# Alternating two products on TensorE: the output product's head pairs and the values product's quarters in the local attention block

## The reference

```
bk2, bv2 = look(bk), look(bv)             # each window of 32 tokens sees itself and the one before
sim  = einsum('bhwie,bhwje->bhwij', bq, bk2) * QK_SCALE   # 16 heads of 64, after l2norm and rotary
attn = softmax(where(mask, -max, sim))
out  = einsum('bhwij,bhwje->bhwie', attn, bv2)             # the values product
x    = out.reshape(b, n, 1024) @ Wo + x                    # the output product
x    = ffn_layer(shift_tokens(x), ...) + x                 # layernorm, 128 -> 2 x 341 -> 128
```

## Time and profile before

| what | value |
| --- | --- |
| median of three timed runs | 4304.2 us |
| the profiled execution's own time | 4290.83 us |
| its span, first to last instruction | 4289.1 us |
| TensorE busy (matmul) | 4007.8 us, 93% |
| VectorE, GpSimd, ScalarE busy | 3256.0, 2944.0, 2597.3 us |
| granted TensorE clock, mean | 0.976 |
| stages loc0 and loc1 | about 1540 us each |

### The profile page before, as it was taken

How to read it: one execution, slowest core, us unless ns; L and a number is a source line. 1 busy time by engine, 2 the same in 40 slices (tenths; PEclk the granted TensorE clock), 3 DMA queues, 4 the chain that set the end, 5 groups by cost and what they waited for, 6 DMA issues and landing times. The chain is left out here.

```text
span 4289.1 us, 151479 instructions
## 1 busy us (share of the span) xinstructions
PE 4007.8 (93%) x66856; PEld 2950.2 (69%) x66856; DVE 3256.0 (76%) x3915; ACT 2597.3 (61%) x3040; POOL 2944.0 (69%) x3505
## 2 busy tenths in 40 slices
PE   8989969999999999999878887799999999999998
PEld 5655557787777787877633333677778777777775
DVE  4535568887888888888668884788888888887885
ACT  4525436666667667667537774466666666666664
POOL 2202168888888888888534441788888888888884
PEclk9999989999999999999989998899999999999999
DMA  4304233233333323322100000333323333232221
GB/s 154 123 10 155 96 100 85 72 88 83 80 84 86 82 76 90 89 66 76 40 11 1 1 1 8 113 81 81 87 79 85 85 85 86 75 87 75 75 65 41
DMA packets 169725, 316.93 MB, mean 74 GB/s; under 512 B 39336, under 2 KB 43056, under 8 KB 166640
## 3 DMA queue, kind: packets, MB, share of 16 engines
q1 hardware_dynamic: 153520, 241.18, 20.7%
q0 software_dynamic: 15552, 66.07, 5.0%
HBM read 92.03 MB, written 20.05 MB: 26 GB/s over the span
## 5 line engine op out<-in xcount | busy, mean ns | idle before, releaser
L694 PE MATMUL psum<-loc_w_hl,loc_z_lo 128*128 128x512 f32 x1152 | 510.0, 443 | 32.5 <-DMA loc_w_hl<-parted 25.9
L941 ACT ACTIVATE loc_sq<-psum 128x1024 f32<-128x1024 f32 x192 | 196.6, 1024 | 459.7 <-PE psum L696 454.6
L1187 DVE TENSOR_REDUCE loc_ssq<-loc_sq 128x16 f32<-128x1024 f32 x384 | 464.1, 1208 | 4.5 <-POOL loc_rn L1076 4.5
L1080 POOL TENSOR_TENSOR loc_rc_k<-loc_rc_k,loc_rs_k 128x1024 f32<-128x1024 f32 x192 | 454.2, 2366 | 19.0 <-DVE loc_rs_k L1201 19.0
L695 PE MATMUL psum<-loc_w_hl,loc_z_hi 128*128 128x512 f32 x1152 | 456.9, 397 | 2.2 <-issue 2.0
L696 PE MATMUL psum<-loc_w_hl,loc_z_hi 128*128 128x512 f32 x1152 | 457.2, 397 | 0.0
L1080 POOL TENSOR_TENSOR loc_rc_q<-loc_rc_q,loc_rs_q 128x1024 f32<-128x1024 f32 x192 | 456.8, 2379 | 0.0
L1099 POOL TENSOR_TENSOR loc_prob<-loc_prob,loc_recip 128x1024 f32<-128x1024 f32 x192 | 365.5, 1904 | 92.1 <-DVE loc_recip L1224 90.5
L791 PE MATMUL psum<-loc_PT,loc_V 64*64 64x32 f32 x24576 | 405.1, 220 | 8.6 <-issue 8.0
L791 PEld LDWEIGHTS psum<-loc_PT,loc_V 64*64 64x64 f32 x24576 | 381.1, 135 | 34.7 <-issue 11.0
L1182 DVE TENSOR_TENSOR loc_rc_q<-psum,loc_rot 128x1024 f32<-128x1024 f32 x192 | 234.9, 1223 | 213.9 <-ACT loc_sq L936 184.0
(11 more groups left out here) (198 smaller groups left out, 9598.4 us busy)
## 6 DMA issues: line engine op xcount, KB each, us to landing
loc_V<-loc_V SPq DMA_DIRECT2D x1152, 128.0 KB
loc_V<-loc_V SPq DMA_DIRECT2D x672, 64.0 KB
loc_w_hl<-parted POOLq DMA_DIRECT2D x72, 512.0 KB, 4.4
parted<-moe_halves POOLq DMA_DIRECT2D x18, 1024.0 KB, 5.2
moe_spread<-moe_gates SPq DMA_DIRECT2D x64, 256.0 KB, 4.0
moe_raw<-in_wqkv POOLq DMA_DIRECT2D x18, 512.0 KB, 6.1
moe_w<-in_moe_w SPq DMA_DIRECT2D x32, 256.0 KB, 3.4
loc_wo<-in_wo SPq DMA_DIRECT2D x12, 512.0 KB, 4.9
```

Source lines behind the costliest of these rows:

```text
L694: pe.matmul(M.bank[bank + g], z_lo[:, r, tokens], w[:, 0, cols], start=True, stop=False)
L1080: pool.tensor_tensor(rc, rc, rs[:, :], ALU.add).then_inc(added, 1)
L1187: dve.tensor_reduce(ssq[:, a:a + HEADS], heads(sq[:, :]), AX_X, ALU.add).then_inc(totalled, 1)
```

## The change

`values` and `output` are each cut in two: one function that holds the waits (`await_values`, `await_output`) and one that issues the part m of the matmuls. Part m of `output` is the pair of head pairs 2m and 2m + 1 (two matmuls, four passes), part m of `values` is a quarter (16 matmuls, 32 passes). In `step` the parts alternate. Waits, operands, banks and the number of matmuls are the same; the semaphores `pv_full` and `y_full` are still raised by the last part.

```
-            def output(L, t):
+            def await_output(L, t):
...
+            def output(L, t, m):
+                for p in (2 * m, 2 * m + 1):
                     mm = pe.matmul(M.bank[ZB][:, 0:P], wo[:, p, :], outT[:, p // (PAIRS // 2), p % (PAIRS // 2), :],
-                                   start=(p == 0), stop=(p == PAIRS - 1))
-                mm.then_inc(y_full, 1)
+                                   start=(p == 0), stop=(p == PAIRS - 1), skip_group_check=True)
+                if m == PAIRS // 2 - 1:
+                    mm.then_inc(y_full, 1)
...
                 if live(n - 4):
-                    output(L, n - 4)
+                    await_output(L, n - 4)
+                    output(L, n - 4, 0)
                 if live(n - 3):
-                    values(L, n - 3, live(n - 1))
+                    await_values(L, n - 3, live(n - 1))
+                for m in range(PAIRS // 2):
+                    if live(n - 4) and m:
+                        output(L, n - 4, m)
+                    if live(n - 3):
+                        values(L, n - 3, m)
```

More of the change, by code:

```diff
@@ L775, in turn_probs, with await_values @@
                 turn(XB, prob, pt_full)
-            def values(L, t, follows):
-                i, b = t % TILES, (L * TS + t) % KEPT
+            def await_values(L, t, follows):
+                i = t % TILES
                 if follows:
@@ L785, in values @@
                 pe.sem_inc(pe_passed, 1)
[L786 to L794, removed]
-            def output(L, t):
+            def values(L, t, m):
+                b = (L * TS + t) % KEPT
+                for w in range(TILES):
+                    for j in range(2):
+                        for c in range(2):
+                            r, q, p = 64 * c, 32 * w, 2 * m + j
+                            mm = pe.matmul(M.bank[WB + c][64 * j:64 * j + 64, m * P + q:m * P + q + 32],
+                                           V2[r:r + 64, b, w, p * 64:(p + 1) * 64], PT[r:r + 64, p, q:q + 32],
+                                           start=True, stop=True, skip_group_check=True)
+                if m == PAIRS // 2 - 1:
+                    mm.then_inc(pv_full, 1)
+            def await_output(L, t):
                 i, s = t % TILES, t // TILES
@@ L809, in output @@
                     pe.wait_ge(hid_ready, upto_seq(L, s - 1, FBLK) - 2)
-                for p in range(PAIRS):
+            def output(L, t, m):
+                for p in (2 * m, 2 * m + 1):
                     mm = pe.matmul(M.bank[ZB][:, 0:P], wo[:, p, :], outT[:, p // (PAIRS // 2), p % (PAIRS // 2), :],
-                                   start=(p == 0), stop=(p == PAIRS - 1))
-                mm.then_inc(y_full, 1)
+                                   start=(p == 0), stop=(p == PAIRS - 1), skip_group_check=True)
+                if m == PAIRS // 2 - 1:
+                    mm.then_inc(y_full, 1)
             def mean(L, t):
```

## The result

The changed kernel takes 4478.52 us at the median (4474.38 to 4481.12, four runs), the kernel before in the same comparison 4306.65 us (4294.06 to 4309.8). The ratio is 1.0405, 95% interval 1.0379 to 1.0431: 172 us more, between 163 and 186. Slower was forecast with 91%, but at +110 us and with a range that ended at 4455. The mechanism was the one named, and its price per pair of borders (0.22 us) was a third too low.

The account below looks back on a forecast made before the run. TensorE's own stream was taken to bound the kernel. Borders +127, holes -14 and slack -3 us gave +110 on the 4304 us median: 4414 us, 2.6% slower, range 4345 to 4455 us.

Parts of the forecast that it names:

- The work and what sets the pace: Local stages: matmul work unchanged, TensorE's own stream sets the pace, both functions live in 190 steps.
- The entry at 0.10 us: Going from output's full array to values' 64 x 64 tiles costs about 0.10 us beyond the pass spacing.
- Coming back about 0.13: Going from values' 64 x 64 tiles back to the full array costs about 0.13 us.
- the blocks' term: Output and values: three more entries and exits a step, 190 x 0.667 = +127 us, bounds 125 to 154.
- The give-back of 17 us: Time returned by vanishing issue holes in values and by slack in waits for other engines: -14 and -3 us.
- The holes in values: TensorE's issue idle within values blocks, 8.0 us in the profile, should go: -14 us, bounds 0 and 19.
- The waits for other engines: TensorE's waits for GpSimd and ScalarE shrink when TensorE is slower: -3 us, bounds 0 and -10.
- Rival (a): Alternating output and values: weight loads run under other passes, borders cost nothing, 4287 us, 0.4% faster; chance 5%.
- (b): Scores: their issue holes go as well, some 60 us, giving 4354 us; chance 8%.
- (c): Output and projection: granted clock falls in one step of five, adding 66 us, 4480 us; chance 7%.
- (d): add_attention or copy_out: a cover is thinner, half the steps pay 0.4 us, 38 us, 4452 us; chance 8%.
- The moved waits: await_values ahead of three quarters of output costs nothing; the query rotation ended 2.1 us before output started.

Follow-up runs that it names:

- narrow_wo: The changed kernel with 96 of Wo's 128 columns as weights of output, a quarter of the output features left out: 4445.03 us in one run.
- halves: The changed kernel with output and values alternating in two parts instead of four: 4356.01 us, ratio 1.0120 to the kernel before.
- eighths_wide: The changed kernel with eight alternating parts instead of four, all four 64 x 64 tiles in use: 4700.78 us, ratio 1.0930 to the kernel before.
- same_shape: Against the kernel before, output's parts 0 to 2 between project_k's passes, part 3 behind, values whole: 4360.46 us, ratio 1.0118.
- output_first: The kernel before with output whole moved in front of project_k, then values: 4430.2 us, ratio 1.0292.
- waits_first: The changed kernel with await_output and await_values in front, then output whole and values whole: 4301.42 us, ratio 0.9994 to the kernel before.

## Why the prediction was wrong in size and right in kind

- The work and what sets the pace: right. TensorE's stream sets the pace, and 190 steps carry the change.
- The entry at 0.10 us, the drain of the exit at 0.13: right (0.54 and 0.60 us for the first part and the quarter, forecast at 0.54 and 0.59). "Coming back about 0.13" is the step that failed, the term of the sum that was mis-sized: coming back costs 0.13 for the drain and 0.10 to 0.11 for a weight load that no running matmul hides, 0.24 in all. Three a step, 190 steps: 3 x 0.107 x 190 = 61 us. With it the blocks' term is 188 instead of 127. I had bounded the exit by the gap before the next block and called the upper end 154 us; the bound was of a wrong distance, so it bounded nothing. The weight loads' rows and narrow_wo show what the missing part is, halves and eighths_wide that the price is fixed, same_shape that it takes a change of tile shape.
- The give-back of 17 us: its size about right, its make-up wrong, so that the sum fits by luck. The holes in values were sized at 14 us; start to start they fell from 10.9 us (13 of them) to 3.0, so 8. The waits for other engines were put at 3 us with 10 as the bound; those for GpSimd before L701 alone fell by 14. In the two traces the local stages differ by 175 us, 13 less than the blocks' 188; the traces as wholes differ by 190, 15 of it outside the stages that the change touches (the mean clock over the whole run is 0.971 after, 0.976 before). The medians differ by 172.
- The idle for issue before the scores was left at its 49.6 us, and with four parts it is (50.4). No rule for it comes out of the runs: 59.2 us with two parts, 36.1 with eight, but 39.8 in output_first, where nothing alternates.
- Rival (a), borders without price: excluded. (b), the scores' holes go: not with four parts. (c), the clock: the stage keeps 0.99. (Its price was read a little low: in the earlier trace rows the granted clock is 0.5 only up to 1233.59, so the 2.43 us of output there are half at either level.) (d), thin covers: none on TensorE. VectorE's add_attention waits for output 38.0 us (13 times) instead of 14.3 (4 times), and no wait of TensorE for another engine grew by more than 2 us.
- The moved waits at nothing: right, by waits_first.

By the Trainium skill, "TensorEngine Tiling (Array Packing)", Key Properties, a change of tiling mode drains TensorE; the runs agree, and same_shape shows the other side, that alternation without such a change costs nothing. The page names no price. Here the drains are 0.10 and 0.13 us, and the load behind the exit comes on top.

## What to carry to other kernels

Read a border between two blocks of TensorE from the last pass of the one to the second pass of the other, not to the first: the first hides a weight load that ran under nothing. Keep passes of one tile shape together, since every there-and-back costs some 0.33 us here, but don't put several blocks of small passes in a row either. In the kernel before, all 64 holes of over 0.4 us within a block of small passes stand behind 74 or more of its 128 passes; with 256 in a row nearly every block had one, of over a us as a rule. A projection that feeds the longest chain on other engines should not be delayed to tidy up TensorE.

## What was not expected of the hardware

- 256 small float32 passes in a row (512 instructions with their loads) had a hole in nearly every step, 1.33 us visible in the one shown, 274.9 us in all; blocks of 128 values passes had 8.0 us in the whole kernel before, those of 128 scores passes 49.6.
- Alternating two full-array products, even between the passes of one accumulation each, cost nothing: 3.33 against 3.37 us.
- With 96 instead of 128 weight columns the passes stayed 0.11 us apart, while the extra behind the exit shrank from 0.102 to 0.078 us.
